# Late experts' words: from a wait before each row load to a wait of TensorE once per four blocks

## The reference

```
h = layernorm(x) * (1 + ca) + sa
x = x + ga * attention(h, W_qkv, b_qkv, W_out, b_out)
h = layernorm(x) * (1 + cb) + sb
scores = softmax(h @ gate_w.T)                 # [tokens, 16]
keep the 2 best of 4 groups of experts, then the 4 best experts, weights normalised
out = sum over e of cw[:, e] * (silu(h @ up_gate[e].T) * (h @ up[e].T)) @ down[e].T
out = out + shared expert(h)
x = x + gb * out
```

## Time and profile before

| | |
|---|---|
| median of 3 runs | 628.28 us (626.14 to 631.13) |
| the profiled execution's own time | 624.17 us |
| its span in the trace | 622.4 us |
| mean granted clock of TensorE | 0.979 |
| matmuls busy (PE) | 571.9 us, 92% |
| weight loads busy (PEld) | 389.7 us |
| VectorE (DVE) busy | 472.3 us, 76% |
| ScalarE (ACT) busy | 373.4 us, 60% |
| GpSimd (POOL) busy | 340.6 us, 55% |
| expert blocks (first L2506 to last) | about 439.4 to 603.9 us |

### The profile page before, as it was taken

The page is one execution under the profiler, slowest core; times in us unless marked ns, Lnnn a source line. Parts: engine busy times, 40 slices in busy tenths (PEclk is TensorE's granted clock), DMA queues, the critical chain, the costliest instruction groups (busy, mean ns, idle before and its releaser), DMA issues. The chain is left out here.

```text
span 622.4 us, 13834 instructions
## 1 busy us (share of the span) xinstructions
PE 571.9 (92%) x4003; PEld 389.7 (63%) x4003; DVE 472.3 (76%) x1401; ACT 373.4 (60%) x877; POOL 340.6 (55%) x646
## 2 busy tenths in 40 slices
PE   8997999999999999998987798899979999999995
PEld 8885533434343444444342386687779999999981
DVE  5858988988888769777948559788866667766756
ACT  4765566766676656555857563554456666666660
POOL 5004662656567455855648876783145555565551
PEclk9979999999999999999999979989999999999998
DMA  8479569873438381852115143664797444444796
GB/s 286 117 201 261 141 142 224 222 174 95 157 87 234 101 217 47 177 186 82 75 52 182 61 166 113 253 206 155 257 400 209 129 138 139 138 128 138 280 341 227
DMA packets 65891, 107.96 MB, mean 173 GB/s; under 512 B 13705, under 2 KB 52377, under 8 KB 64026
## 3 DMA queue, kind: packets, MB, share of 16 engines
q1 hardware_dynamic: 58954, 87.93, 48.2%
q0 software_dynamic: 6864, 19.15, 7.9%
HBM read 60.90 MB, written 43.88 MB: 168 GB/s over the span
## 5 line engine op out<-in xcount | busy, mean ns | idle before, releaser
L1459 ACT ACTIVATE Pr<-bank 128x512 f32<-128x512 f32 (+3 forms) x384 | 165.7, 494 | 95.9 <-PE bank L2261 91.6
L1575 DVE TENSOR_REDUCE mxA<-bank 128x1 f32<-128x128 f32 (+3 forms) x256 | 112.2, 483 | 20.0 <-PE bank L2146 19.7
L2261 PE MATMUL bank<-Qs,Ks 99*128 99x512 bf16 (+3 forms) x384 | 117.0, 328 | 5.6 <-ACT Pr L1459 4.3
L1281 POOL DMA_INDIRECT expert_rows<-Y,YIX x79 | 77.2, 977 | 79.1 <-ACT Y L1522 76.8
L2146 PE MATMUL bank<-Ks,Qs 96*128 96x512 bf16 (+3 forms) x384 | 119.1, 327 | 1.3 <-DVE mxB L1575 0.6
L1575 DVE TENSOR_REDUCE mxB<-bank 128x1 f32<-128x512 f32 x128 | 81.7, 682 | 13.4 <-PE bank L2146 13.3
L2247 PE MATMUL bank<-Pr,Vst 128*32 128x512 f32 (+3 forms) x768 | 82.0, 499 | 3.5 <-POOL Pr L1260 3.5
L1258 POOL TENSOR_TENSOR tick<-ident 128x1 f32<-128x1 f32 x128 | 25.4, 198 | 104.3 <-ACT Pr L1459 103.4
L1210 POOL DMA_INDIRECT chosen_rows<-Hx,pos x64 | 67.6, 1056 | 20.8 <-issue 18.5
L2506 PE MATMUL bank<-W,xh 128*128 x316 | 78.0, 328 | 0.9 <-issue 0.9
L2261 PEld LDWEIGHTS bank<-Qs,Ks 99*128 99x128 bf16 x384 | 35.7, 97 | 57.6 <-ACT Pr L1459 39.0
(11 more groups left out here) (255 smaller groups left out, 1268.9 us busy)
## 6 DMA issues: line engine op xcount, KB each, us to landing
G<-chosen_rows SPq DMA_DIRECT2D x79, 134.0 KB, 2.2
W<-expert_words SPq DMA_DIRECT2D x7, 1088.0 KB, 8.9
qk_parts<-AP SPq DMA_DIRECT2D x32, 192.0 KB, 3.0
Z<-expert_rows SPq DMA_DIRECT2D x12, 512.0 KB, 6.7
Wraw<-in_wexp SPq DMA_DIRECT2D x9, 608.0 KB, 6.0
SA<-in_wexp SPq DMA_DIRECT2D x7, 608.0 KB, 5.5
Vst<-Vall SPq DMA_DIRECT2D x8, 512.0 KB, 6.4
expert_words<-SH SPq DMA_DIRECT2D x7, 480.0 KB, 2.8
```

Of the source, the lines that this page charges most:

```text
L1281: nc.gpsimd.indirect_dma_start(out=zd, out_offset=bass.IndirectOffsetOnAxis(ap=YIX[:, b:b + 1], axis=0), in_=Y[b % YRING], in_offset=None) ...
L1459: nc.scalar.activation(Pr[(2 * s + j // 2) % 4][:, j % 2, 0:w], ebank[p % RING][:, 0:w], ACT.Exp, scale=SCALE).then_inc(exp_done, EXP)
L1575: nc.vector.tensor_reduce(dst, mbank[u % RING][:, 0:w], AX.X, ALU.max).then_inc(m_red, 1)
L2261: nc.tensor.matmul(ebank[p % RING][:, 0:CH - q0], Ks[slot][0:NAUG, j, kt * P:(kt + 1) * P], Qs[slot][0:NAUG, qc, j, q0:CH], start=True, st ...
```

## The change

Four things change together.

- `ebt` gets 20 groups of five numbers. Four are the block experts as before; the fifth, written by one more VectorE instruction, is max(1, last expert of the group - 7): how far the semaphore `late_words` must have come for that group.
- SP raises `late_words` once before block 0 and once for each late expert's words that it has seen landed.
- `load_block` waits for no landed words; the wait is done at a block of its own (`READY_AT`), four blocks behind the one that issues the load (`FINAL_AT`). The seven loads are issued behind blocks 8, 10, 12, 14, 16, 18 and 20.
- TensorE loads five numbers instead of four for the groups that begin at blocks 0 to 24, and waits for `late_words` to reach the fifth. At block 28 it waits for the constant 8. `s_assert_within` puts a check of the register's bounds into the instruction stream.

```diff
-BLOCK_SP = {7: [("final", 11), ("final", 12)], 9: [("final", 13)], 10: [("final", 14), ("final", 15)], 11: [("final", 16)], 12: [("final", 17)]}
+FINAL_AT = {PRE + i: 8 + 2 * i for i in range(NPRE)}
+READY_AT = {_k: _s + 4 for _k, _s in FINAL_AT.items()}
+READY_ALL = -(-(max(READY_AT.values()) + 1) // IDX_LOAD) * IDX_LOAD
+FIRST_LATE = PRE - NSH
+GROUPS, GROUP = (NB + 1) // IDX_LOAD, IDX_LOAD + 1
...
-        ebt = rows.put("ebt", [1, NB + 1], I32)
+        ebt = rows.put("ebt", [1, GROUPS, GROUP], I32)
...
                 sp.wait_ge(w_lo, NSH + min(b, PRE - NSH - 1) + 1)
-                if PRE <= b + NSH < NW:
-                    sp.wait_ge(w_raw[b + NSH], WORDS_IN)
...
+            sp.sem_inc(late_words, 1)
             for b in range(NB):
                 load_block(b)
-                for piece in BLOCK_SP.get(b, ()):
-                    work(piece)
+                for k in range(PRE, NW):
+                    if FINAL_AT[k] == b:
+                        load_final(k)
+                    if READY_AT[k] == b:
+                        sp.wait_ge(w_raw[k], WORDS_IN)
+                        sp.sem_inc(late_words, 1)
...
-                dve.wait_ge(tab_ready, TAB_STEPS - 1)
-                nc.vector.scalar_tensor_tensor(out=ebt[0:1, :], in0=experts, scalar=NE - 1.0, in1=moved,
-                                               op0=ALU.min, op1=ALU.add).then_inc(tab_ready, 1)
+                dve.wait_ge(tab_ready, TAB_STEPS - 2)
+                grouped = "o (g k) -> o g k"
+                nc.vector.scalar_tensor_tensor(out=ebt[0:1, :, 0:IDX_LOAD], in0=experts.rearrange(grouped, k=IDX_LOAD), scalar=NE - 1.0,
+                                               in1=moved.rearrange(grouped, k=IDX_LOAD), op0=ALU.min, op1=ALU.add).then_inc(tab_ready, 1)
+                nc.vector.tensor_scalar(ebt[0:1, :, IDX_LOAD:GROUP], experts.rearrange(grouped, k=IDX_LOAD)[:, :, IDX_LOAD - 1:IDX_LOAD],
+                                        2.0 - FIRST_LATE, 1.0, ALU.add, ALU.max).then_inc(tab_ready, 1)
...
                     n = min(IDX_LOAD, NB - u)
+                    more = u < READY_ALL
                     _, values = nc.values_load_multi_w_load_instructions(
-                        ebt[0:1, u:u + n], engines=(mybir.EngineType.PE,), min_val=0, max_val=NE - 1,
+                        ebt[0:1, u // IDX_LOAD, 0:n + more], engines=(mybir.EngineType.PE,), min_val=0, max_val=NE - 1,
...
-                    expert.update({u + k: v for k, v in enumerate(values)})
+                    expert.update({u + k: v for k, v in enumerate(values[:n])})
+
+                    if more:
+                        pe.wait_ge(late_words, nc.s_assert_within(values[n], 1, 1 + NPRE))
+                    elif u == READY_ALL:
+                        pe.wait_ge(late_words, 1 + NPRE)
```

More of the change, by code:

```diff
@@ L322 @@
 BLOCK_DVE = {1: [("lo", 10)]}
-BLOCK_SP = {7: [("final", 11), ("final", 12)], 9: [("final", 13)], 10: [("final", 14), ("final", 15)], 11: [("final", 16)], 12: [("final", 17)]}
-for _table, _lead in ((BLOCK_DVE, 5), (BLOCK_SP, NSH + 1)):
-    assert all(_s <= _p[1] - _lead for _s in _table for _p in _table[_s])
+assert all(_s <= _p[1] - 5 for _s in BLOCK_DVE for _p in BLOCK_DVE[_s])
+FINAL_AT = {PRE + i: 8 + 2 * i for i in range(NPRE)}
+READY_AT = {_k: _s + 4 for _k, _s in FINAL_AT.items()}
+READY_ALL = -(-(max(READY_AT.values()) + 1) // IDX_LOAD) * IDX_LOAD
+FIRST_LATE = PRE - NSH
+assert all(_s <= _k - NSH + GRING - 2 for _k, _s in READY_AT.items())
+assert (NB + 1) % IDX_LOAD == 0
+GROUPS, GROUP = (NB + 1) // IDX_LOAD, IDX_LOAD + 1
 MIN_NEEDED = T * TOPK // P
@@ L619, in program @@
         tab_ready = sem("tab_ready")
+        late_words = sem("late_words")
         prow_ready = sem("prow_ready")
@@ L687, in read_of @@
             return bank_read[USE[piece][0]]
-        TAB_STEPS = 2 + 2 * len(PLACE_STEPS)
+        TAB_STEPS = 3 + 2 * len(PLACE_STEPS)
         assert sum(Z_PARTS) <= PRE
@@ L1040, in work @@
                     load_words(piece[1])
-                if piece[0] == "final":
-                    load_final(piece[1])
             for s in range(-1, SN):
```

## The result

| | before | changed |
|---|---|---|
| median of 6 runs | 627.21 us (624.60 to 631.13) | 634.73 us (631.14 to 637.67) |
| ratio, 95% interval | | 1.0133 [1.0097, 1.0169] |
| profiled execution, its span | 624.17, 622.4 us | 637.67, 635.9 us |
| block phase (first L2506 or L2523 matmul of block 0 to that of block 78) | 163.4 us | 172.4 us |

The change is slower by 7.5 us where 2.6 less was forecast. The profiled execution of the changed kernel is the slowest of its six, 13.5 us over that of before. Of these, 9.0 lie in the block phase and 2.8 ahead of it, where the granted clock from 300 to 400 us was 0.90 against 0.97. Behind it lie 1.7. Only the block phase is compared from here on.

A forecast was written before the change was run, and what follows sets the result against it. TensorE was taken to set the pace past block 16, with a hole at blocks 9 to 12. Terms -5.3 + 2.4 + 0.15 + 0.15 + 0.05 = -2.6 us gave a median of 625.7 us, range 621.8 to 629.5.

The forecast's parts named there:

- What bounds the kernel: Block phase: TensorE alone sets the pace past block 16, with one hole at blocks 9 to 12.
- part 1: SP's row loads no longer wait for words, so the lost time at blocks 9 to 12 goes: -5.3 us.
- The hole of 5.3 us: Blocks 9 to 12: time TensorE lost waiting for rows of blocks 11 to 13, with slow issue behind each wait.
- SP's waits at the ready points: On SP, short waits at the ready points were to replace L1028's wait of 15.4 us.
- Part 2: TensorE's sequencer, blocks 4 to 24: fifth number, check and wait cost 0.4 us a group, 2.4 us in all.
- the longer load: 0.012 a word: TensorE's register load: the fifth number adds 0.012 us, from 0.305 for four words against 0.268 for one.
- The check and the wait: TensorE's sequencer, each group of five: check 0.197 + 0.068 us and wait 0.101 us, gaps included.
- Part 3: The start: block 0's longer load mostly covered, 0.15 us; VectorE's additional instruction 0.15; block 28's constant wait 0.05.
- TensorE's sequencer becomes the bound at every group: Rival, all groups of five: register check and wait empty the matmul queue; 629.3 us at the high end, chance 0.10.
- Its point of decision, 0.77 us a group: Groups of five on TensorE: the cost per group at which the sequencer rival decides, (5.3 - 0.3) / 6.5.
- The second rival: DMA queue: rows stay late through full engines, taking back 2.9 us, additions 2.8; 628.0 us, no change; chance 0.10.
- Block 21 at 482: Row loads: at 5.0 us a pair, block 21's rows come at 482, 2.9 us late; kept for the range.

The follow-up runs named there:

- e3_rows_only: The changed kernel with only SyncE's new load order; table, VectorE step and TensorE's four-number loads as before, one constant wait at block 28: ratio 0.9879, phase 157.5 us.
- e2_stride5: The kernel before with only the table's layout changed, groups of four numbers 20 bytes apart: ratio 1.0114, phase 172.4 us.
- e1_pad8: The changed kernel with its groups of five numbers 32 bytes apart instead of 20: ratio 0.9937 of before, phase 160.8 us.
- e11_shift4: The kernel before with its table begun 4 bytes later, groups still 16 bytes apart: phase 173.3 us, 636.98 us once.

## Why the prediction was wrong

- **What bounds the kernel, and part 1** held. The hole of 5.3 us was a wait for row loads held behind words, and it goes: e3_rows_only is 5.9 us shorter in the phase, no row is late. One reading in it was wrong and did no harm: SP's waits at the ready points were to be short and are as long as before (7 of them, 16.3 us), but TensorE waits for no row behind them:

```profile
SPq L1058 <- DMA W<-expert_words: 16.3, 7, 3.6
```

- **Part 2 is the step that failed**, in it the term "the longer load: 0.012 a word". It came from the difference of a load of four (0.305) and of one (0.268). Both are one fetch, so the difference is no price of a word. The fifth number is a second fetch, 0.25 us, and at 15 of 20 groups the distance of 20 bytes made every number one. The groups of five cost 7.2 us where 2.4 were counted; on multiples of 16 bytes they would have cost 3.2.
- **The prediction left a term out**: it priced the fifth number and did not price the layout. The groups from block 28 on load four numbers as before and were taken as untouched; they cost 5.2 us. e2_stride5 shows that the layout alone is enough to lose as much as the change did (1.0114 against 1.0133). With the layout put right (e1_pad8) the phase is 2.6 us shorter, the very figure of the forecast, and that is partly luck: the loads' new order gives 5.9 where 5.3 were counted, and the groups of five take 3.2 where 2.4 were.
- **The check and the wait** were counted at 0.37 us and are about 0.25. That the sequencer has nothing to spare at a group was right: the excess follows the length of the load almost one for one (a load 0.67 us longer costs 0.6).
- **The rule I set aside.** I wrote that the trace disagrees with the Trainium skill's "Runtime: NRT & Kernel Launch", section "Instruction fetch mechanics", about 200 ns for a register. I compared only four numbers with one. A third case stood in the earlier trace rows, the longest load, 772 ns, and I took it for one of four numbers. It is the last one, of three (blocks 76 to 78), and so took over twice as long as four:

```profile
L2499 PEldq TENSOR_LOAD <-ebt x1: 772/772/772, 598.0 to 598.0; - x1
```

That alone spoke against 0.012 a word. For a number by itself these runs give some 0.25 us (0.77 for three, 1.00 for four), so there the rule is near; it is far off for four numbers on a multiple of 16 bytes, 0.33 in all.
- **Part 3** was right in size for VectorE: the new instruction takes 0.17 us, and block 0's longer load (0.79 for 0.52) lies ahead of the phase, whose first three intervals then take 0.13 less, so most of it is covered. Block 4's is not, 0.9 us even when aligned (3.94 against 3.00).
- **The rival** that TensorE's sequencer becomes the bound at every group named the right place and the right sign. The reason that it gave, the check and the wait, was not the one: they cost about 0.25 us, and the load did the rest. Its point of decision, 0.77 us a group, was passed at five of six groups of five. I gave it 0.10, because the median load took 0.33 us, and took that as the price of any load of this kind.
- **Slips in the sums.** They change little. The second rival adds up to -5.3 + 2.9 + 2.8 = +0.4, so 628.7 and not 628.0. Block 21 at 482 would be 2.6 us late by the figures shown, not 2.9. The spread of 5 us is that of the three single runs, not of medians. The range was to be widened by 1.5 us at both ends and got 1.2 at the upper one.

## What to carry to other kernels

A table that a sequencer reads in groups of four 4-byte numbers should have each group on a multiple of 16 bytes; adding one column to it can make every read of it three times as long, also the reads that the column does not concern. Where an engine bounds the kernel, its sequencer's loads and checks belong to its time: put them on an engine that stands idle, at the place in its order where it does. A price taken from the difference of two durations holds only while both cross the same steps, so ask what the next size crosses.

## What the runs showed of the hardware

- Register loads from SBUF: 0.33 us for four numbers on a multiple of 16 bytes, 0.59 for five or eight, 0.77 for three, 1.00 for four elsewhere, 1.29 to 1.64 for five elsewhere, on TensorE's sequencer; ScalarE's load of one took 0.28. A distance of 8 bytes from a multiple of 16 is as slow as 4 (the groups of e2_stride5 begin 0, 4, 8 and 12 bytes behind one).
- After 1.57 us of idle at block 4 the changed kernel's granted clock was 0.76 and then 0.81 in two windows of four us, a mixture of TensorE's two levels, 1.2 and 2.4 GHz: from 452.2 to 455.4 us it was 0.50, the lower level, and 1.00 from 448 to 452 and from 455.6 to 460. The block took 3.50 us. e2_stride5 and e11_shift4 had loads of 1.32 us at the same place and no such fall (2.09 us); what brings it on is open.
